# GpSimd's product with C in a selective scan: one instruction per unit of two steps instead of one per step

## The chip, the cores and the metric

The kernel runs on one core of one Trainium2 chip. The metric is device time in microseconds from start to end of one launch. The core has four computing engines with queues of their own: TensorE (PE), VectorE (DVE), ScalarE (ACT) and GpSimd (POOL). SyncE (SP) issues most transfers. An engine works its queue strictly in order; between engines only semaphores order the work.

## The reference, cut to what matters

Two layers run one after the other on a tensor of 32 x 96 x 56 x 56, all in f32. The first is a 7x7 depthwise convolution with a layer norm and an MLP. The second cuts the image into windows of 8 x 8 pixels and runs a two-dimensional selective scan in each, in four directions:

```
def step(h, inp):
    u_l, d_l, B_l, C_l = inp
    dA = jnp.exp(d_l[..., None] * A)
    h = h * dA + (d_l * u_l)[..., None] * B_l[:, :, None, :]
    y = jnp.einsum('bkdn,bkn->bkd', h, C_l)
    return (h, y)
```

Here d is 192 channels, n is 16 states per channel, k is 4 directions, and l runs over the 64 pixels of a window. delta (d_l) is softplus of a small product of the input. The change touches the product of h with C_l; its sum over n is another instruction.

## The kernel before, in words

**Tiles and turns.** layer0 comes first. layer1 then works on 196 tiles of 8 windows (512 pixels, `TOK`). Each engine has a function `body(b)`, which is one turn of 48 steps (`STEPS1`); turn b scans tile b, prepares parts of tile b+1, and finishes tile b-1. A turn has two phases (f = 0, 1: by rows and by columns) of 24 steps (`SPP`). Two successive steps, the even one and the odd one (s = 0, 1), are a unit; `unit(p)` gives a step's phase, its block J of 32 channels, its direction pair h, its slot and s. A unit's state, 128 x 2048 values, lies in one of six slots of the tile `state`.

**One step p, engine by engine.** ACT writes the decays exp(d A) into the slot four steps ahead (`decays`, L1256, two instructions a step). PE writes the step's inputs, 32 small matmuls, into one of two PSUM tiles dbu (`inputs`, L1032). It waits there for the scan of two steps before. DVE runs the recurrence in place over the 1024 columns of the step (`scan`, L1477). POOL multiplies these by C in place (`times_c`, L942); it waits for the step's scan and counts the product on `hc_done`. PE sums the states of a whole unit over n into the bank yb (`sum_states`, L1051), five steps after the unit's odd step (`LAG`); ACT copies the bank out. The sum counts on `ysum_done`, for which the decays of the unit six later wait.

**The chain of a step size.** Six times a turn (`CHAINS`, at steps 5, 12, 19, 33, 40 and 47) a block of 64 channels gets its delta. PE multiplies (`steps_of`, L1120) into the one bank pp that all side work shares; ACT takes absolute value, relu and exponential of it (`softplus`, L1325, L1326, L1328), then two logarithms (L1333, L1334). PE sums those three steps later (`exponent`, L1126) and ACT takes an exponential (`small_part`, L1339). Five steps after the chain's start, POOL adds (`step_size`, L949, counts `dl_done`), multiplies by u (`times_u`, L962 or L964, counts `hd_done`) and writes resets (L973, counts `reset_done`). The result goes through DRAM into dl, from which the decays are taken. PE transposes the product with u eight steps after the chain's start (`inputs_turned`, L1133) and ACT copies it (L1347) into du_t, which `inputs` reads. The softplus of a chain waits for `dl_done` of the chain before it. POOL also has one product a turn at step 35 (`gate`, L978).

**Where these sit in POOL's queue.** In step p, `times_c` comes first, then the chain's three instructions if p is 4, 10, 17, 24, 38 or 45, then at p = 35 the gate.

**Side work on pp.** The matmuls on pp go in a fixed order (`PP`). Each waits until the one before it has been read (`free_bank`), so L1100, the second depthwise convolution of the next tile (in steps 21 and 24, read by ACT in L1280, L1281, L1284), waits for L1347 of the transposition before it, and L1126 of step 22 waits for L1284.

**C and its loads.** SP brings C spread over partitions into cc, 2 h x 2 s x 1024 columns, a unit's 2048 columns of one h in one contiguous row (`c_rows`). It may overwrite a half h when `hc_done` shows that the last unit of that h in the phase is through (`LAST_STEP` = 18 for h = 0, 22 for h = 1). The first products of a phase on each h wait for the load (`cc_in`).

Of the kernel before, what the change touches and what calls it, by code (L numbers as in the profile page):

```python
# [7 lines left out]
ALU = mybir.AluOpType  # L8
# [33 lines left out]
WPS = TW // 2  # L42
# [5 lines left out]
LAST_STEP = [18, 22]  # L48
UPP = len(PHASE_J)
SPP = 2 * UPP  # L50
UNITS = 2 * UPP
STEPS1 = 2 * SPP
# [502 lines left out]
def layer1(nc, ln_g, ln_b, in_w, conv_w, conv_b, xproj_w, dt_w, dt_b, A_logs, Ds, on_g, on_b, out_w, alpha,  # L555
           act_d, base_d, cd, out, NT):
    ctx = ExitStack()
    with ctx:
        def sb(name, shape, dt=F32):
            return ctx.enter_context(nc.sbuf_tensor(name, shape, dt))  # L560
# [4 lines left out]
        def sem(name):  # L565
            return ctx.enter_context(nc.semaphore(name))
# [55 lines left out]
        cc = sb("cc", [128, 2, 2, STEP])  # L622

        state = sb("state", [128, NSLOT, TW, MG * WPX])
# [28 lines left out]
        cc_in = [sem(f"cc_in{h}") for h in range(2)]  # L653
# [10 lines left out]
        CCS = NG * 16  # L664
        STORES = TW * 16

        def later(t):
            return not (isinstance(t, int) and t == 0)
# [33 lines left out]
        def unit(p):  # L702

            f, of_phase = p // SPP, p % SPP // 2
            return f, PHASE_J[of_phase], PHASE_H[of_phase], p // 2 % NSLOT, p % 2
# [30 lines left out]
        with nc.Block() as block:  # L736

            @block.sync
            def _(sp):
# [10 lines left out]
                with nc.allow_non_contiguous_dma(reason="small weights, once"):  # L750
# [7 lines left out]
                    for part, (rows, first) in enumerate(PARTS):  # L758
                        its = slice(first, first + rows)
# [81 lines left out]
                def c_rows(T, f, h):  # L841

                    phase = T * 2 + f
                    if h == 0:
                        sp.wait_ge(cd_in[f], T * CDS + CDS)
                    if later(phase):
                        sp.wait_ge(hc_done, phase * SPP + (LAST_STEP[h] + 2 - SPP))
                    for g in range(NG):
                        src = cd[f, h].rearrange("s w g m t -> g (s w) (m t)")[g]
                        sp.dma_start(cc[JC * g:JC * g + JC, h, :, :].rearrange("p s (w x) -> p (s w) x", w=WPS),  # L850
                                     src.unsqueeze(0).broadcast_to([JC, TW, MG * WPX])).then_inc(cc_in[h], 16)

                def body(b):
                    if has(b):
                        c_rows(b, 0, 1)
# [7 lines left out]
                    if has(b):  # L863
                        both_halves(b, 1, 1)
                        c_rows(b, 1, 0)
                        c_rows(b, 1, 1)
                        both_halves(b, 1, 2)
# [29 lines left out]
            def _(pool):  # L897
# [37 lines left out]

                def times_c(b, p):
                    f, _, h, slot, s = unit(p)
                    pool.wait_ge(scan_done, b * STEPS1 + p + 1)
                    if p % SPP in (0, 4):
                        pool.wait_ge(cc_in[h], (b * 2 + f + 1) * CCS)  # L940
                    its = state[:, slot, WPS * s:WPS * s + WPS, :].rearrange("p w x -> p (w x)")
                    nc.gpsimd.tensor_tensor(its, its, cc[:, h, s, :], ALU.mult).then_inc(hc_done, 1)  # L942

                def step_size(T, f, j):

# [34 lines left out]
                def body(b):  # L980
                    for p in range(STEPS1):
                        if has(b):
                            times_c(b, p)
                        for T, f, j in chains_at(b, p, L_U):
                            step_size(T, f, j)
                            times_u(T, f, j)
                            reset(T, f, j)
                        if p == S_GATED and has(b - 1):
                            gate(b - 1)
# [10 lines left out]
            def _(pe):  # L1000
# [41 lines left out]
                def sum_states(T, p):  # L1042

                    f, J, h, slot, _ = unit(p)
                    bank = yb[J % 2]
                    pe.wait_ge(hc_done, T * STEPS1 + p + 1)
                    if h == 0 and (later(T) or 6 * f + J > 1):
                        pe.wait_ge(ye_done, T * (2 * NJC) + 6 * f + J - 1)
                    for m in range(MG):
                        src = state[:, slot, :, m * WPX:m * WPX + WPX].rearrange("p (q k) t -> p k q t", k=2)  # L1050
                        last = nc.tensor.matmul(bank[JC * m:JC * m + JC, :].rearrange("p (k q t) -> p k q t", k=2, t=WPX),  # L1051
                                                mask[:], src[:, ::-1, ::-1, ::-1] if h else src, start=h == 0, stop=h == 1)
                    if f == 0 and h == 0:
                        for m in range(MG):
                            its = slice(128 * m, 128 * m + 128)
                            last = nc.tensor.matmul(bank[JC * m:JC * m + JC, its],
                                                    skip_l[:, J // 2, JC * (J % 2):JC * (J % 2) + JC],
                                                    u[0:JB, J // 2, its], start=False, stop=False)
                    last.then_inc(ysum_done, 1)
# [145 lines left out]
                def body(b):  # L1205
                    for p in range(STEPS1):
                        T, q = (b, p + 1) if p < STEPS1 - 1 else (b + 1, 0)
                        done = b if p >= LAG else b - 1
                        if has(T):
                            inputs(T, q, 0)  # L1210
                        if has(done) and (p - LAG) % 2:
                            sum_states(done, (p - LAG) % STEPS1)
                        if has(T) and NE > 1:
                            first_halves_written(T, q)
                            inputs(T, q, 1)
                        front(b, p)
# [348 lines left out]
```

## Time and profile before

| | us |
|---|---|
| median of 3 runs | 31036.96 (31032.65 to 31046.93) |
| span of the profiled execution | 31035.4 |

No separate time of the profiled execution is on record; its span, from the first to the last instruction, lies within the three runs. Times in the views are microseconds from the start of that span. Busy is the share of the span in which an engine ran something; a line of a timeline merges neighbouring instructions of one line of code (x2, x6), with the idle time ahead of them in brackets and the engine and line whose end closed it. PE's share of 92% counts modelled ends of pipelined matmuls. Layer0 fills roughly the first 3.4 ms, in which POOL is idle nearly throughout.

### The profile page before, as it was taken

The page shows a single profiled execution, that of the slowest core. Times are in us where ns is not written, and L with a number is a line of the kernel's source. Part 1 is how long each engine was busy: PE and PEld are TensorE (multiplying, and loading weights), DVE is VectorE, ACT ScalarE, POOL GpSimd, SP SyncE. Part 2 cuts the span into 40 slices and gives each one's busy share as a digit, 9 for nine tenths or more (in the row PEclk, how much of TensorE's full clock was granted, in tenths as well). Part 3 has the DMA queues.
Part 4 walks back from the last instruction along what each step waited for, and adds up shares of the span by engine and source line. Part 5 has one row for each costly group of instructions (what it writes and reads, how often), then busy time and mean ns, then how long its engine had stood idle before and what let it go on. Part 6 is the DMA issues. An engine that isn't in the chain of part 4 may idle for free.

```text
span 31035.4 us, 986155 instructions
## 1 busy us (share of the span) xinstructions
PE 28615.5 (92%) x399070; PEld 10807.2 (35%) x399070; DVE 27602.9 (89%) x18447; ACT 24152.4 (78%) x37826; POOL 25853.7 (83%) x13288
## 2 busy tenths in 40 slices
PE   8999799999999999999999999999999999999998
PEld 2333233333333333333333333333333333333333
DVE  7888799999999999999999999999999999999998
ACT  4555688888888888888888888888888888888887
POOL 0000599999999999999999999999999999999999
PEclk9999999999999999999999999999999999999999
DMA  3333344444444444444444444444444444444444
GB/s 82 88 84 82 79 103 99 102 98 102 99 101 100 100 100 100 101 100 102 99 102 100 101 99 101 99 103 98 103 98 102 100 102 99 102 98 102 98 102 90
DMA packets 3821867, 3043.32 MB, mean 98 GB/s; under 512 B 2184848, under 2 KB 2987792, under 8 KB 3796944
## 3 DMA queue, kind: packets, MB, share of 16 engines
q1 hardware_dynamic: 3809888, 2910.77, 44.4%
q8 instruction: 3312, 54.26, 0.8%
q0 software_dynamic: 8560, 77.41, 0.7%
q14 instruction: 107, 0.88, 0.0%
HBM read 2325.71 MB, written 449.58 MB: 89 GB/s over the span
## 4 chain that ended last, share of the span: by engine, by line
PE 28%; POOL 20%; issue 18%; ACT 13%; DVE 8%; DMA 1%; POOLq 0%; SPq 0%; ACTq 0%; DVEq 0%
POOL state L942 17%; PE dbu L1032 9%; PE pp L1126 7%; DVE state L1477 5%; ACT state L1256 5%; PE yb L1051 4%; DVE dg L1467 2%; PE pp L1100 2%; POOL dd L949 2%; PE pp L1089 1%; PE pp L1120 1%; ACT sp_w L1333 1%; POOL dd L962 1%; ACT sp_v L1334 1%; PE b_t L1068 1%
## 5 line engine op out<-in xcount | busy, mean ns | idle before, releaser
L942 POOL TENSOR_TENSOR state<-state,cc 128x1024 f32<-128x1024 f32 x9408 | 22044.2, 2375 | 1411.5 <-DVE state L1477 1381.9
L1477 DVE TENSOR_TENSOR_SCAN state<-state,dbu 128x1024 f32<-128x1024 f32 x9408 | 21000.9, 2269 | 2295.8 <-PE dbu L1032 2292.6
L1256 ACT ACTIVATE state<-dl,a_neg 128x512 f32<-128x512 f32 x18816 | 12250.6, 711 | 21.2 <-DMA dl<-dlx 1.4
L1032 PE MATMUL dbu<-dg,du_t 64*32 64x256 f32 x301056 | 10198.2, 383 | 968.5 <-DVE state L1477 895.6
L1032 PEld LDWEIGHTS dbu<-dg,du_t 64*32 64x32 f32 x301056 | 5100.0, 106 | 7276.9 <-issue 6198.1
L1051 PE MATMUL yb<-state,mask 128*32 128x512 f32 x37632 | 5078.5, 612 | 2.2 <-POOL state L942 2.2
L1467 DVE TENSOR_TENSOR dg<-b_t,mask_q 128x1024 f32<-128x1024 f32 x3136 | 3757.7, 1198 | 41.4 <-PE b_t L1068 41.4
L229 POOL DMA_DIRECT2D act_d<-acted x32 | 16.3, 509 | 3218.2 <-DVE mixed L489 2909.2
L1126 PE MATMUL pp<-sp_a,minus 128*128 128x512 f32 x2352 | 1321.4, 644 | 587.4 <-ACT ye L1284 252.1
L1339 ACT ACTIVATE sp_y<-pp 128x512 f32<-128x512 f32 x1176 | 704.2, 599 | 1440.4 <-PE pp L1126 1417.1
L437 DVE SCALAR_TENSOR_TENSOR acc<-image,cw_v,acc 96x432 f32<-96x432 f32 (+2 forms) x2912 | 1687.6, 647 | 0.0
L262 PE MATMUL conv_p<-shifted,cw 128*32 128x424 f32 (+3 forms) x12096 | 1646.1, 542 | 0.4 <-DVE b1g L406 0.4
L949 POOL TENSOR_TENSOR dd<-sp_r,sp_y 128x512 f32<-128x512 f32 x1176 | 1507.9, 1282 | 111.3 <-ACT sp_y L1339 111.3
L1051 PEld LDWEIGHTS yb<-state,mask 128*32 128x32 f32 x37632 | 743.7, 108 | 1962.1 <-issue 1783.5
L1120 PE MATMUL pp<-xd,dt_l 128*128 128x512 f32 x2352 | 1324.4, 645 | 102.9 <-ACT xd L1308 81.5
L1126 PE MATMUL pp<-sp_w,minus 128*128 128x512 f32 x2352 | 1202.8, 593 | 0.0
L1126 PE MATMUL pp<-sp_v,minus 128*128 128x512 f32 x2352 | 1202.5, 593 | 0.0
L1347 ACT ACTIVATE du_t<-pp 128x512 f32<-128x512 f32 x1176 | 683.7, 581 | 541.2 <-PE pp L1133 540.6
L1325 ACT ACTIVATE sp_a<-pp 128x512 f32<-128x512 f32 x1176 | 698.9, 594 | 516.2 <-POOL dd L949 271.3
L1100 PE MATMUL pp<-xs,cw 96*32 96x448 f32 (+1 forms) x7056 | 1009.1, 563 | 12.7 <-DMA xs<-ye 9.1
L1308 ACT ACTIVATE xd<-pp,one_row 64x512 f32<-64x512 f32 x784 | 535.6, 683 | 608.4 <-PE pp L1109 603.4
L964 POOL TENSOR_TENSOR dd<-dd,u 128x512 f32<-128x512 f32 x588 | 902.7, 1535 | 92.7 <-POOL dd L949 62.1
(174 smaller groups left out, 26584.2 us busy)
## 6 DMA issues: line engine op xcount, KB each, us to landing
dl<-dlx SPq DMA_DIRECT2D x4704, 256.0 KB, 4.7
cc<-cd SPq DMA_DIRECT2D x3136, 256.0 KB, 6.2
dlx<-dd SPq DMA_DIRECT2D x1176, 256.0 KB, 2.0
shifted<-in_x SPq DMA_DIRECT2D x384, 392.0 KB, 12.5
xs<-ye SPq DMA_DIRECT2D x1176, 112.0 KB, 2.8
xs<-ye SPq DMA_DIRECT2D x588, 128.0 KB, 2.6
image<-in_x SPq DMA_DIRECT2D x32, 1176.0 KB, 24.5
act_d<-acted POOLq DMA_DIRECT2D x32, 1176.0 KB, 9.1
```

The source lines that it names most:

```text
L262: last = nc.tensor.matmul(dst[:, :, lo:hi], cw[:, cb * PCOLS + w, :], src.rearrange("p (i j) -> p i j", j=W)[:, :, lo + e:hi + e], start=t ...
L437: nc.vector.scalar_tensor_tensor(dst, src, weight, dst, ALU.mult, ALU.add).then_inc(tap_done, 1)
L942: nc.gpsimd.tensor_tensor(its, its, cc[:, h, s, :], ALU.mult).then_inc(hc_done, 1)
L949: nc.gpsimd.tensor_tensor(dd[:, 0, :], sp_r[:], sp_y[:], ALU.add).then_inc(dl_done, 1)
L1032: last = nc.tensor.matmul(dst[:, :, TQ * e:TQ * e + TQ], du_t[its, j, col:col + JC], dg[its, h, 2 * k + s, MG * TQ * g:MG * TQ * g + MG * ...
L1051: last = nc.tensor.matmul(bank[JC * m:JC * m + JC, :].rearrange("p (k q t) -> p k q t", k=2, t=WPX), mask[:], src[:, ::-1, ::-1, ::-1] if ...
L1100: last = nc.tensor.matmul(windows(pp[32 * q:32 * q + 32, :])[:, :, :, a:c], cw[:, 3 * cb + d, :], windows(xs[:, 2 * (cb % 3) + cb // 3, :] ...
L1120: nc.tensor.matmul(pp[:], dt_l[:, f, j, :], xd[:, f, :], start=True, stop=True).then_inc(pp_ready, 1)
L1126: last = nc.tensor.matmul(pp[:], minus[:, i, :], part[:], start=i == 0, stop=i == 2)
L1256: nc.scalar.activation(state[:, slot, :, m * WPX:m * WPX + WPX].rearrange("p (q k) t -> p q k t", k=2), by_place(dl[:, J // 2, 2 * h + J % ...
L1467: nc.vector.tensor_tensor(dg[:, h, blk, :].rearrange("p (n t) -> p n t", t=TQ), b_t[:, col:col + NS].unsqueeze(2).broadcast_to([128, NS, TQ]),
L1477: nc.vector.tensor_tensor_scan(its, its, dbu[p % 2][:], 0.0, ALU.mult, ALU.add).then_inc(scan_done, 1)
```

## The change

`times_c` does nothing on an even step. On an odd step it waits for the scan of that step (so for both), and multiplies the unit's 2048 columns by the 2048 columns of C in one instruction. `hc_done` counts units instead of steps; the two places that wait for it (`c_rows` on SP, `sum_states` on PE) count units too, and wait for the same data as before. The waits for `cc_in` move from steps 0 and 4 of a phase to steps 1 and 5.

```diff
@@ c_rows
                     if later(phase):
-                        sp.wait_ge(hc_done, phase * SPP + (LAST_STEP[h] + 2 - SPP))
+                        sp.wait_ge(hc_done, phase * UPP + (LAST_STEP[h] // 2 + 1 - UPP))
@@ times_c
                     f, _, h, slot, s = unit(p)
+                    if s == 0:
+                        return
+                    if p % SPP in (1, 5):
+                        pool.wait_ge(cc_in[h], (b * 2 + f + 1) * CCS)
                     pool.wait_ge(scan_done, b * STEPS1 + p + 1)
-                    if p % SPP in (0, 4):
-                        pool.wait_ge(cc_in[h], (b * 2 + f + 1) * CCS)
-                    its = state[:, slot, WPS * s:WPS * s + WPS, :].rearrange("p w x -> p (w x)")
-                    nc.gpsimd.tensor_tensor(its, its, cc[:, h, s, :], ALU.mult).then_inc(hc_done, 1)
+                    its = state[:, slot, :, :].rearrange("p w x -> p (w x)")
+                    nc.gpsimd.tensor_tensor(its, its, cc[:, h, :, :].rearrange("p s x -> p (s x)"),
+                                            ALU.mult).then_inc(hc_done, 1)
@@ sum_states
-                    pe.wait_ge(hc_done, T * STEPS1 + p + 1)
+                    pe.wait_ge(hc_done, T * UNITS + p // 2 + 1)
```

## Rows read from the trace of the kernel before

**Rows 1.** The page: busy us (share of span) and instructions of each engine.

```profile
PE 28615.5 (92%) x399070; PEld 10807.2 (35%) x399070; DVE 27602.9 (89%) x18447; ACT 24152.4 (78%) x37826; POOL 25853.7 (83%) x13288
```

**Rows 2.** The page: shares of the chain that ended last, by line.

```profile
POOL state L942 17%; PE dbu L1032 9%; PE pp L1126 7%; DVE state L1477 5%; ACT state L1256 5%; PE yb L1051 4%; DVE dg L1467 2%; PE pp L1100 2%; POOL dd L949 2%; PE pp L1089 1%; PE pp L1120 1%; ACT sp_w L1333 1%; POOL dd L962 1%; ACT sp_v L1334 1%; PE b_t L1068 1%
```

**Rows 3.** POOL's groups: shapes, xcount | busy us, mean ns | idle before, releasers.

```profile
L942 POOL TENSOR_TENSOR state<-state,cc 128x1024 f32<-128x1024 f32 x9408 | 22044.2, 2375 | 1411.5 <-DVE state L1477 1381.9 <-DMA cc<-cd 23.4
L949 POOL TENSOR_TENSOR dd<-sp_r,sp_y 128x512 f32<-128x512 f32 x1176 | 1507.9, 1282 | 111.3 <-ACT sp_y L1339 111.3
...
L973 POOL TENSOR_TENSOR dd<-resets 128x8 f32<-128x8 f32 x1176 | 245.1, 208 | 176.0 <-POOL dd L962 89.5 <-POOL dd L964 63.9 <-ACT state L1256 6.5
```

**Rows 4.** Line L978, once a turn: duration min/median/max ns, first and last start.

```profile
L978 POOL TENSOR_TENSOR yf<-yf,z x196: 2340/2365/2394, 3700.0 to 31021.8; 128x1024 f32<-128x1024 f32 x196
```

**Rows 5.** Waits over the span: waiter, releaser, us in total, times, longest.

```profile
ACT sp_a L1325 <- POOL dd L949: 271.3, 198, 3.2
```

**Rows 6.** Timeline of POOL in one turn, steps 3 to 17: start, duration.

```profile
11895.22 4.70 POOL L942 TENSOR_TENSOR state<-state,cc 128x1024 f32<-128x1024 f32 x2 [0.94 <-DVE state L1477]
11899.88 1.27 POOL L949 TENSOR_TENSOR dd<-sp_r,sp_y 128x512 f32<-128x512 f32 x1
...
11902.92 14.01 POOL L942 TENSOR_TENSOR state<-state,cc 128x1024 f32<-128x1024 f32 x6
11916.89 1.29 POOL L949 TENSOR_TENSOR dd<-sp_r,sp_y 128x512 f32<-128x512 f32 x1
...
11920.18 16.36 POOL L942 TENSOR_TENSOR state<-state,cc 128x1024 f32<-128x1024 f32 x7
11936.49 1.28 POOL L949 TENSOR_TENSOR dd<-sp_r,sp_y 128x512 f32<-128x512 f32 x1
11937.93 1.56 POOL L964 TENSOR_TENSOR dd<-dd,u 128x512 f32<-128x512 f32 x1 [0.16 <-PE pp L1120]
```

**Rows 7.** Timeline of DVE, same turn: scans 3 and 4, scan 17, scan 24.

```profile
11892.86 4.46 DVE L1477 TENSOR_TENSOR_SCAN state<-state,dbu 128x1024 f32<-128x1024 f32 x2
...
11929.08 2.29 DVE L1477 TENSOR_TENSOR_SCAN state<-state,dbu 128x1024 f32<-128x1024 f32 x1 [1.45 <-PE dbu L1032]
...
11952.95 2.29 DVE L1477 TENSOR_TENSOR_SCAN state<-state,dbu 128x1024 f32<-128x1024 f32 x1 [1.65 <-PE dbu L1032]
```

**Rows 8.** Timeline of ACT, same turn: softplus of steps 5 and 19, then L1347.

```profile
11901.25 0.60 ACT L1325 ACTIVATE sp_a<-pp 128x512 f32<-128x512 f32 x1 [1.31 <-POOL dd L949]
...
11937.92 0.60 ACT L1325 ACTIVATE sp_a<-pp 128x512 f32<-128x512 f32 x1 [0.26 <-PE pp L1120]
...
11941.28 0.58 ACT L1347 ACTIVATE du_t<-pp 128x512 f32<-128x512 f32 x1
```

**Rows 9.** Timeline of PE, same turn, steps 16 to 23.

```profile
11928.73 1.07 PE L1051 MATMUL yb<-state,mask 128*32 128x512 f32 x8
...
11940.25 0.66 PE L1133 MATMUL pp<-ident,dd 128*128 128x128 f32 x4
11941.53 1.10 PE L1032 MATMUL dbu<-dg,du_t 64*32 64x256 f32 x32 [0.63 <-DVE state L1477]
11942.56 2.57 PE L1100 MATMUL pp<-xs,cw 96*32 96x512 f32 x24
...
11948.80 1.12 PE L1126 MATMUL pp<-sp_a,minus 128*128 128x512 f32 x2 [1.29 <-ACT ye L1284]
```

**Rows 10.** Timeline of ACT in the rest of the same turn, step 32.

```profile
11980.67 1.38 ACT L1308 ACTIVATE xd<-pp,one_row 64x512 f32<-64x512 f32 x2 [1.25 <-PE pp L1109]
```

**Rows 11.** Timeline of PE in the rest of the same turn, step 43.

```profile
12008.37 1.12 PE L1126 MATMUL pp<-sp_a,minus 128*128 128x512 f32 x2 [0.71 <-ACT zi L1315]
```

**Rows 12.** Timeline of DVE, scan of the same turn's last step.

```profile
12019.19 2.29 DVE L1477 TENSOR_TENSOR_SCAN state<-state,dbu 128x1024 f32<-128x1024 f32 x1 [0.26 <-PE dbu L1032]
```

**Rows 13.** Timeline of DVE, scan of step 3 in a longer turn.

```profile
12596.14 2.28 DVE L1477 TENSOR_TENSOR_SCAN state<-state,dbu 128x1024 f32<-128x1024 f32 x1
```

**Rows 14.** Timeline of ACT, softplus of step 19 in that longer turn.

```profile
12642.38 0.60 ACT L1325 ACTIVATE sp_a<-pp 128x512 f32<-128x512 f32 x1 [0.26 <-PE pp L1120]
```

## The prediction

> **What bounds the kernel now.** I read the page's busy line first. PE is at 92%, DVE 89%, POOL 83%, ACT 78% [rows 1]; no engine is full, so the time is set by hand-overs inside a turn, not by one sum of busy time. The span holds 196 turns; the gate runs once in each, from 3700.0 to 31021.8 us [rows 4], so a turn takes 27,321.8 / 195 = 140.1 us. Whatever the change does, it does about 196 times, and 1 us a turn is 196 us.
>
> Then the chain's lines. POOL's product has the largest share, 17% [rows 2]. This must not be read as 17% to be won or lost. Over the whole span DVE is what POOL waits for, 1381.9 us [rows 3]; an engine that is often early is not the one that sets the pace. What counts are the points where another engine waits for POOL. The list of waits has one of any size: ACT's softplus for the `step_size`, 271.3 us in 198 waits, about one a turn [rows 5]. The timelines of one turn show which: the softplus of step 5 starts at 11901.25, after 1.31 us of idle that POOL ends [rows 8], as POOL's L949 ended at 11899.88 + 1.27 = 11901.15 [rows 6]. POOL's other wait in that place is for scan 3: it stands idle for 0.94 us, until scan 3 has ended at 11892.86 + 2.27 = 11895.13 [rows 6, 7]. So scan 3, two products, step size, softplus is a piece of the turn's pace.
>
> The second place is the softplus of step 19. It starts at 11937.92, put down to PE [rows 8], but POOL's L949 ended only at 11936.49 + 1.28 = 11937.77 [rows 6]: POOL is 0.15 us from being the bound. From 11895.22 to there POOL has no idle but the 0.16 us steps inside a chain's three instructions. Its work between scan 3 and step 17 is a solid block, and how long the new block is decides the result.
>
> **What one merged product costs.** The trace has no POOL product of 2048 columns. It has 128x512 at 1.282 us, 128x1024 at 2.375 and 128x8 at 0.208 [rows 3]. From 512 to 1024 columns is 1.093 us; twice that for 1024 more gives 2.375 + 2.186 = 4.561. The line from 8 to 1024 columns, 2.133 ns a column, gives 2.375 + 1024 x 2.133 ns = 4.559. I take 4.56. The bounds: from above twice today's, 4.75; from below, the slope of the two large shapes with no fixed part at all, 2048 x 2.135 ns = 4.37. Products in a row start closer than their duration: seven take 16.36 us [rows 6], so (16.36 - 2.375) / 6 = 2.33 each, 0.04 less than one lasts. A merged one then occupies 4.52 where a pair took 4.66, 0.14 less.
>
> The Trainium skill has a measured figure for just this shape: GPSIMD Engine Reference, section 3.1 (Elementwise, side-by-side cycle accounting), gives 4497 ns for a tensor_tensor of 2048 f32, an add. No row here shows it. By it the sum below would end at no loss a turn.
>
> **The change part by part.** POOL loses 4704 of 9408 products [rows 3], busy time 4704 x (2 x 2.375 - 4.56) = 890 us. None of it counts in itself, as POOL waits for DVE anyhow. What counts is when the consumers get their data.
>
> Step 4 (the known wait). Before, products 3 and 4 ran before the step size. Now step 4 has no product, and the unit of 2 and 3 starts after scan 3, at the same 11895.22, and lasts one merged product. L949 starts at 11895.22 + 4.52 = 11899.74 in place of 11899.88: 0.14 us earlier.
>
> Step 17 (the near miss). Here the chain sits in an odd step, right behind a merged product. Block before, from product 3: L949 at 11899.88, products again at 11902.92, L949 at 11916.89, products at 11920.18, L949 at 11936.49 [rows 6]. The chain's three instructions hold POOL 3.04 and 3.29 us. After: 11899.74 + 3.04 = 11902.78; three units (5, 7, 9), 13.56, to 11916.34; + 3.29 = 11919.63; four units (11 to 17), 18.08, to 11937.71. That is 1.22 us later than 11936.49. In words: the block holds eight whole units where it held fifteen products, so half a unit (2.33) comes in, the half that had been done while DVE scanned step 3, and eight savings of 0.14 go out. The scans don't hold this block: scan 17 ends at 11929.08 + 2.29 = 11931.37 [rows 7], the product of its unit starts at 11933.2.
>
> What follows it. L949 ends at 11938.99; with the 0.10 us that ACT took at step 5 the softplus starts at 11939.09, 1.17 after 11937.92. ACT is without a gap until L1347, so that ends at 11941.28 + 0.58 + 1.17 = 11943.03. `times_u` ends at 11937.93 + 1.56 + 1.22 = 11940.71, and PE's transposition, at 11940.25 before [rows 9], comes at about 11940.8 and is done before 11941.53, when PE starts the inputs it had waited 0.63 us for a scan to begin [rows 9]. So that wait swallows PE's part. ACT's part isn't swallowed whole: the convolution L1100 must not overwrite pp before L1347 has read it; it began at 11942.56 [rows 9], 0.70 after L1347's end, and would now begin at about 11943.10. Net: 1.22 - 0.05 - 0.70, plus 0.07 for the hand-over, = 0.54 us.
>
> Does this reach the end of the turn? L1100 releases ACT's four reads, L1284 releases L1126 after 1.29 us of idle on PE [rows 9], then come the inputs for scan 24, for which DVE idles 1.65 us [rows 7]. All of that moves by 0.54. Further on the hand-overs stay tight: ACT idle 1.25 for L1109, PE idle 0.71 for ACT's L1315, DVE idle 0.26 for PE ahead of scan 46 [rows 10 to 12]. I find no slack that gives it back, and scan 3 of the next turn starts the same block anew.
>
> Longer turns. PE's loop is written out eight turns at a time, and about one turn in eight (24) is longer. In one of them scan 3 ends at 12598.42 and the softplus of step 19 starts 43.96 later, at 12642.38 [rows 13, 14], in place of 42.79. The new L949 ends 43.86 after scan 3, so it costs nothing there. The sum: 172 turns x 0.54 = 93 us more, 24 x 0.14 = 3 us less: +90 us on 31,035.4, which is 31,125. The profiled span lies 1.6 us under the median of the runs, so no correction.
>
> **The edits at no cost.** The steps 10, 24, 38: their chains come at the same time or earlier, since they sit in even steps; step 45 is odd, and by the same sum its step size comes at most half a unit, 2.33 us, later. The 198 waits of softplus for L949 are one a turn and the one of step 5 is among them [rows 5, 8], so I take the softplus of step 47 to have room for it; if it had none, 1 us a turn more. `sum_states` takes the unit of 10 and 11 at 11928.73 [rows 9]; its product ends at 11919.63 + 4.56 = 11924.19, 4.5 us ahead. If that cover went, each of 24 sums a turn would stop PE. The `cc` reload waits for the same unit, which is done 1 us later and has its load needed one scan later; SP's queue behind it (the next chain's store) then waits no longer either. The decays hang on the sums and don't move.
>
> **The rivals.**
> 1. Not slower: the merged product is shorter than 4.49. Every 0.01 us counts eight times in the block, so the 0.54 is gone when a unit lasts 0.0675 less, 4.49; the place is L1347's 0.70 us ahead of L1100. Below it the gain is what step 4 wins, 2 x 2.33 less the unit's spacing: at 4.37, 0.33 us a turn, 65 us, 30,970. Against: three shapes of this trace on one line at 4.56. At 4.49 itself the time is 31,035 to 31,000. 18%, of which 8% for more than 62 us. (The Trainium skill's figure of GPSIMD Engine Reference, section 3.1, lies on this point.)
> 2. The instruction saves nothing (4.75). The block grows by 8 x 0.19 = 1.5 more: 2.05 us x 172 = 350 us: 31,390. For it only that a fixed part may be charged per 1024 columns. 8%.
> 3. The delay is real but given back behind L1100, by a slack I don't see: 31,035. Against it stand the tight hand-overs [rows 10 to 12]. 17%.
> 4. A consumer of whole units becomes late after all (`sum_states`, or cc through SP's queue), once or twice a turn by about a us: + 200 to 400 us. Against it the 4.5 us. 7%.
> Forecast: 50%.
>
> **How the numbers follow.** A difference under 0.2%, 62 us, can't be told from none here. The forecast holds +90 with a spread of about 60 (0.04 us on the product is 55 us), so a third of it falls below 62. Slower: 0.36 + 0.08 + 0.07 + a little of the rest, 0.54; faster 0.09; same 0.37. The range leaves out the far part of rivals 2 and 4 and the lowest of rival 1: 30,995 to 31,280.
>
> **What would show it.** L942 has 4704 instructions of 128x2048 near 4.56 us. The wait of the softplus L1325 for L949 rises from one a turn to about two, and the new one is at step 19, near 1.2 us. In a usual turn L949 of step 17 ends 43.9 us after scan 3, and L1100 starts 0.07 us after L1347's end. PE's sums still don't wait for L942. Wrong would be: L1100 with slack left, a product off 4.56, or DVE idle ahead of scan 24 unchanged while the time moves.

## The result and the profile after

| | before | after |
|---|---|---|
| median of 6 runs, us | 31033.90 (31028.22 to 31046.93) | 31132.83 (31117.82 to 31145.84) |
| span of the profiled execution | 31035.4 | 31116.2 |

The changed kernel takes 1.0029 times as long, 95% interval 1.0020 to 1.0039. The forecast was 31,125. First the page of the changed kernel: busy time by engine, the lines of the chain that ended last, and the group of POOL's product. POOL's product is now L944; line numbers past `times_c` have moved by three (L952 is `step_size`, L1480 the scan).

```profile
PE 28631.3 (92%) x399070; PEld 10810.1 (35%) x399070; DVE 27607.9 (89%) x18447; ACT 24139.7 (78%) x37826; POOL 25167.9 (81%) x8584
...
PE dbu L1035 9%; POOL state L944 8%; PE pp L1129 8%; ACT state L1259 7%; DVE state L1480 7%; PE yb L1054 4%; DVE dg L1470 3%; PE pp L1103 2%; PE pp L1123 2%; POOL dd L952 1%; PE pp L1111 1%; PE pp L1112 1%; ACT xd L1311 1%; ACT du_t L1350 1%; ACT sp_w L1336 1%
...
L944 POOL TENSOR_TENSOR state<-state,cc 128x2048 f32<-128x2048 f32 x4704 | 21347.2, 4559 | 2182.7 <-DVE state L1480 2172.2
```

POOL has 686 us less to do than in [rows 1] and waits 790 us longer for DVE than in [rows 3]; its share of the chain fell from 17% [rows 2] to 8%. By each of these three numbers the change looks like a gain, and the kernel is slower. The list of waits (waiter, releaser, us in total, times, longest) has the one that grew:

```profile
ACT sp_a L1328 <- POOL dd L952: 414.6, 319, 2.9
```

Against [rows 5] that is 121 more waits and 143 us more. Sorted by step, two things hide in this number: the softplus of step 19 waited for POOL once in the whole span before and now does in 187 of 196 turns, and that of step 5 does in 131 turns instead of 196. The timelines of a usual turn show them. POOL, from the product of steps 2 and 3 to the step size of step 17 (start, duration, idle before in brackets):

```profile
12057.94 4.56 POOL L944 TENSOR_TENSOR state<-state,cc 128x2048 f32<-128x2048 f32 x1 [2.06 <-DVE state L1480]
12062.46 1.27 POOL L952 TENSOR_TENSOR dd<-sp_r,sp_y 128x512 f32<-128x512 f32 x1
...
12082.32 18.11 POOL L944 TENSOR_TENSOR state<-state,cc 128x2048 f32<-128x2048 f32 x4
12100.36 1.30 POOL L952 TENSOR_TENSOR dd<-sp_r,sp_y 128x512 f32<-128x512 f32 x1
```

DVE in the same turn, scans 3 and 4:

```profile
12055.58 4.46 DVE L1480 TENSOR_TENSOR_SCAN state<-state,dbu 128x1024 f32<-128x1024 f32 x2
```

Scan 3 ends at 12055.58 + 2.27 = 12057.85, and the step size of step 17 at 12101.66, which is 43.81 us later; before it was 11937.77 - 11895.13 = 42.64 [rows 6, 7]. Before the change POOL stood idle twice, 0.92 us ahead of product 2 and 0.94 ahead of product 3, and did product 2 while DVE scanned step 3:

```profile
11891.91 2.37 POOL L942 TENSOR_TENSOR state<-state,cc 128x1024 f32<-128x1024 f32 x1 [0.92 <-DVE state L1477]
```

Now it stands idle once, for 2.06 us, about the same in all, and product 2 is inside the merged one, behind scan 3: that is the half unit that came into the block. ACT and PE behind the block:

```profile
12101.75 0.60 ACT L1328 ACTIVATE sp_a<-pp 128x512 f32<-128x512 f32 x1 [1.52 <-POOL dd L952]
...
12105.11 0.58 ACT L1350 ACTIVATE du_t<-pp 128x512 f32<-128x512 f32 x1
```

```profile
12104.11 1.10 PE L1035 MATMUL dbu<-dg,du_t 64*32 64x256 f32 x32
12105.82 2.57 PE L1103 MATMUL pp<-xs,cw 96*32 96x512 f32 x24 [0.61 <-ACT du_t L1350]
```

The softplus of step 19, put down to PE before [rows 8], now idles 1.52 us for POOL. The convolution L1103 (L1100 before), which had no idle [rows 9], stands 0.61 us until L1350 has read pp. Over the usual turns (median) scan 24 starts 58.36 us after the end of scan 3, before 57.82, and from scan 24 to the next turn's scan 0 it is 70.01 and 70.02: in such a turn the 0.54 us arise between scans 3 and 24 and nothing behind gives them back. The median turn goes from 140.06 to 140.58 us.

### The profile page after: what moved, and what is told of

The parts are those of the page before. It is cut to its first block, busy times and chain, and to the rows that moved or that the text cites. A ratio compares the mean times of both kernels' runs of the same rounds, so it can differ in the third digit from the quotient of the medians.

```text
span 31116.2 us, 980775 instructions
## 1 busy us (share of the span) xinstructions
PE 28631.3 (92%) x399070; PEld 10810.1 (35%) x399070; DVE 27607.9 (89%) x18447; ACT 24139.7 (78%) x37826; POOL 25167.9 (81%) x8584
## 4 chain that ended last, share of the span: by engine, by line
PE 31%; ACT 19%; issue 17%; DVE 11%; POOL 11%; ACTq 0%; DVEq 0%; SPq 0%; POOLq 0%; DMA 0%
PE dbu L1035 9%; POOL state L944 8%; PE pp L1129 8%; ACT state L1259 7%; DVE state L1480 7%; PE yb L1054 4%; DVE dg L1470 3%; PE pp L1103 2%; PE pp L1123 2%; POOL dd L952 1%; PE pp L1111 1%; PE pp L1112 1%; ACT xd L1311 1%; ACT du_t L1350 1%; ACT sp_w L1336 1%
## 5 line engine op out<-in xcount | busy, mean ns | idle before, releaser
L944 POOL TENSOR_TENSOR state<-state,cc 128x2048 f32<-128x2048 f32 x4704 | 21347.2, 4559 | 2182.7 <-DVE state L1480 2172.2
L1480 DVE TENSOR_TENSOR_SCAN state<-state,dbu 128x1024 f32<-128x1024 f32 x9408 | 21004.8, 2269 | 2358.3 <-PE dbu L1035 2355.4
L952 POOL TENSOR_TENSOR dd<-sp_r,sp_y 128x512 f32<-128x512 f32 x1176 | 1503.7, 1279 | 110.9 <-ACT sp_y L1342 110.9
L1350 ACT ACTIVATE du_t<-pp 128x512 f32<-128x512 f32 x1176 | 682.0, 580 | 556.7 <-PE pp L1136 556.7
L1103 PE MATMUL pp<-xs,cw 96*32 96x448 f32 (+1 forms) x7056 | 1009.2, 563 | 103.7 <-ACT du_t L1350 90.9
L1136 PE MATMUL pp<-ident,dd 128*128 128x128 f32 x4704 | 772.6, 287 | 290.5 <-ACT sp_r L1329 169.3
```

Source lines behind the costliest of these rows:

```text
L944: nc.gpsimd.tensor_tensor(its, its, cc[:, h, :, :].rearrange("p s x -> p (s x)"), ALU.mult).then_inc(hc_done, 1)
L952: nc.gpsimd.tensor_tensor(dd[:, 0, :], sp_r[:], sp_y[:], ALU.add).then_inc(dl_done, 1)
L1103: last = nc.tensor.matmul(windows(pp[32 * q:32 * q + 32, :])[:, :, :, a:c], cw[:, 3 * cb + d, :], windows(xs[:, 2 * (cb % 3) + cb // 3, :] ...
L1480: nc.vector.tensor_tensor_scan(its, its, dbu[p % 2][:], 0.0, ALU.mult, ALU.add).then_inc(scan_done, 1)
```

## The experiments

Each kernel was timed in five rounds beside the kernel before; ratios are to that, with 95% intervals.

**Only the block merged** (`in_block`), and **only the rest merged** (`out_block`). The edit lets `times_c` choose; a merged unit counts two on `hc_done`, so all waits keep their numbers. Counting two has a small price of its own: with all units merged POOL's program has 4,696 more semaphore instructions than the changed kernel's, and the step size of step 17 ends 0.10 us later (43.91 us after scan 3 against 43.81).

```diff
+                    whole = 2 <= p < 18        # out_block: p >= 18
+                    if whole and s == 0:
+                        return
...
+                    if whole:
+                        its = state[:, slot, :, :].rearrange("p w x -> p (w x)")
+                        nc.gpsimd.tensor_tensor(its, its, cc[:, h, :, :].rearrange("p s x -> p (s x)"),
+                                                ALU.mult).then_inc(hc_done, 2)
```

> Only the units of steps 2 to 17 are one instruction; all other steps keep one product each, and hc_done counts steps, so PE's and SP's programs are those of before. Theory (the solid block of POOL between scan 3 and the step size of step 17 is half a unit longer): the whole loss is here, +70 to +115 us against before, ratio about 1.003; the step size of step 17 ends 43.8 us after scan 3. Rival A (PE's register instructions for the new count): no loss, within 20 us of before. Rival B (consumers of whole units outside the block, cc reloads or the odd chain of step 45): half of the loss or less.

> Only the units of steps 18 to 47 are one instruction; steps 0 to 17 keep one product each, counts as before. Theory: no loss, within 20 us of before, though POOL loses 15 of 24 pairs a turn and its busy time falls by some 550 us. Rival B (a consumer of whole units outside the block, or the chain of step 45): +50 to +115 us. Rival A: no loss either.

`in_block`: 31108.56 us, ratio 1.0025 (1.0015 to 1.0034); step size of step 17 at 43.91 us after scan 3. With 8 of 24 units merged the loss is 80 us, as with all of them and the same counting (82, `all_by_two` below). `out_block`: 31386.70 us, 1.0117 (1.0102 to 1.0132), 358 us more than before, which no theory expected. The group of single products shows a releaser that had 23.4 us before [rows 3]:

```profile
L950 POOL TENSOR_TENSOR state<-state,cc 128x1024 f32<-128x1024 f32 x3528 | 8257.0, 2370 | 595.6 <-DVE state L1485 396.5 <-DMA cc<-cd 196.7
```

So the reload of cc is late, for product 4 of a turn, and with it the step size of step 4 (7.24 us after scan 3 in the median turn, before 6.03). The wait for cc is 173 us longer, half of the 358; what makes the rest is seen in the next run.

**Where the late reload comes from.** `out_mid` merges steps 18 to 43 and leaves 44 to 47 single:

```diff
-                    whole = p >= 18
+                    whole = 18 <= p < 44
```

> As the kernel that merges only the units of steps 18 to 47 (which took 358 us more than before), but the last two units of the turn, steps 44 to 47, keep one product a step; merged are steps 18 to 43. Theory C (the 358 us are the reload of cc for h = 1: it goes out behind the transfers of step 45's chain, which a merged unit ahead of it makes 1.2 us later, and product 4 of the next turn, alone in its instruction, needs it at once): no loss, within 25 us of before. Rival D (merged units outside the block cost by themselves, each sum or reload a little): 13 of the 15 units are still merged, so +250 us or more.

31356.44 us, 1.0101 (1.0086 to 1.0117). Theory C in this form fell: the last units were not it. But the test had left the chain of step 45 late, since merged units still stood ahead of it. POOL's timeline in `out_mid`, around a scan 0 that starts at 12131.67:

```profile
12143.97 2.38 POOL L950 TENSOR_TENSOR state<-state,cc 128x1024 f32<-128x1024 f32 x1 [0.59 <-DVE state L1485]
12147.83 2.36 POOL L950 TENSOR_TENSOR state<-state,cc 128x1024 f32<-128x1024 f32 x1 [1.49 <-DMA cc<-cd]
...
12166.19 2.37 POOL L950 TENSOR_TENSOR state<-state,cc 128x1024 f32<-128x1024 f32 x1 [1.35 <-DVE state L1485]
```

The first wait makes the second. Product 4 is late, so the softplus of step 5 is, so PE's work on pp and its inputs are (DVE idles 6.28 us for them ahead of scan 10, in the turn of rows 6 it was 3.11), and POOL waits 1.35 us for a scan in the middle of the block, where it had no idle before [rows 6]. From scan 3 to the end of step 17's step size it is 44.27 us in the median turn, before 42.64.

SP's queue of the same turn: store of the chain and reload of cc.

```profile
12131.73 0.34 SPq L825 DMA_DIRECT2D dlx<-dd  x1
12137.67 1.79 SPq L850 DMA_DIRECT2D cc<-cd  x4
```

The same two before the change, in a turn whose scan 0 starts at 12022.96:

```profile
12021.63 0.34 SPq L825 DMA_DIRECT2D dlx<-dd  x1
12027.01 1.79 SPq L850 DMA_DIRECT2D cc<-cd  x4
```

The store leaves 1.4 us later in the turn, the reload 2 us later (6.0 us into the turn against 4.05; over the turns the medians are 5.69 and 4.00). `out_mid_45` takes only that away: the chain of step 45 stands ahead of product 45.

```diff
-                        if has(b):
+                        if has(b) and not (p == 45):
                             times_c(b, p)
                         for T, f, j in chains_at(b, p, L_U):
                             ...
+                        if has(b) and (p == 45):
+                            times_c(b, p)
```

> Still merged in steps 18 to 43 and single elsewhere (which took 324 us more than before), with one reordering: step 45's chain of three POOL instructions comes ahead of product 45. In that run merged units ahead of the chain had left its reset 1.4 us later than before, its store, its loads and, behind them in SP's queue, the reload of cc 2 us later, and product 4 waited for cc. Theory C' (so it is this chain, not the last unit): the reset comes 1 us earlier than before the change, the reload goes out by 5.5 us into the turn, the waits of POOL for cc go, time within 30 us of before. Rival D (merged units outside the block cost by themselves): +250 us or more.

31031.41 us, 0.9999 (0.9990 to 1.0008), and 13 of 24 units are merged. POOL's wait for cc is back to 15.9 us:

```profile
L950 POOL TENSOR_TENSOR state<-state,cc 128x1024 f32<-128x1024 f32 x4312 | 10094.2, 2376 | 231.6 <-DVE state L1487 214.9 <-DMA cc<-cd 15.9
```

The reload goes out 4.73 us into the median turn. So merged units outside the block cost nothing that these runs resolve (6 us less than before, inside the interval), and the late chain of step 45 does if the first use of cc stays at step 4. In the changed kernel the unit of 4 and 5 starts after the first step size and isn't held up: L944 above has no wait for cc. Nor has `all_by_two`, where the reload leaves as late as in `out_mid`, at 5.91 us.

**The order at step 17** (`chain17_first`: the edit of `out_mid_45`, with 17 for 45, in the changed kernel).

> The changed kernel with one reordering in POOL's queue: in step 17 the chain's three instructions come ahead of the unit's product instead of behind it. Theory: the step size of step 17 comes a unit (4.5 us) earlier, PE is again what the softplus of step 19 waits for, the loss of 0.54 us a turn goes and the 0.14 us of step 4 stays: 20 to 30 us under before, about 31,005. Rivals A and B: still +60 to +115 us against before.

31020.46 us, 0.9998 (0.9989 to 1.0007), and the step size of step 17 ends 39.30 us after scan 3. The loss is gone: 8 us under before, where 20 to 30 were expected, and the interval can't tell these apart. The median turn, 139.99, is 0.07 under that of before, where 0.14 was expected.

**PE's own instructions** (`all_by_two`). The changed `sum_states` makes PE compute a count of its own; the changed kernel runs 4,368 more register instructions there. Here `whole = True` and counts of two leave PE's program as it was.

> As the changed kernel, every unit one instruction, but each counts two on hc_done, so that PE and SP wait for the same numbers and run the same programs as before the change (the changed kernel has some 4,400 more register instructions on PE). Theory: the loss stays, +70 to +115 us, same as the changed kernel. Rival A: it goes, within 20 us of before; a part of it going would be PE's part.

31111.41 us, 1.0026 (1.0016 to 1.0036); median turn 140.66. The loss stays, so most of it isn't PE's. A part may be. PE's pauses ahead of the inputs that no releaser explains (issue) are 77.3 us in 52 waits in the changed kernel, 10.3 in 30 here:

```profile
PE dbu L1035 <- issue: 77.3, 52, 4.0
```

Most fall on step 5, where the softplus then waits for PE in place of POOL. By the medians this kernel is 21 us shorter than the changed one, inside the intervals, though its block is 0.10 us longer by the way it counts, which at 0.10 us a turn would be up to 20 us. So an estimate of PE's part is 20 to 40 us of the 99; no run shows it by itself.

**Half a unit out of the block** (`split_first`: `whole = p // 2 != 1`).

> Every unit one instruction except that of steps 2 and 3, which keeps one product a step. Theory (half a unit too much in POOL's block from scan 3 to step 17): product 2 is done while DVE scans step 3, the step size of step 4 comes about 2.1 us earlier than before the change and that of step 17 about 0.8 us earlier, the loss is gone and PE, not POOL, is waited for at step 5; the gain there ends where PE itself is busy, 0.7 us a turn: 100 to 160 us under before, about 30,900. Rival: if the loss comes from merged units anywhere else, it stays, +60 us or more.

30887.71 us, 0.9953 (0.9939 to 0.9966), as expected. One unit of 24 done in two steps turns a loss of 99 us (82 with the same counting) into a gain of 145: step 4's step size ends 4.09 us after scan 3 where it ended at 6.03 before the change, and step 17's at 42.07 where it was 42.64.

**A dose of POOL time**, one idle product of 128x512, inside the block and outside it:

```diff
                         for T, f, j in chains_at(b, p, L_U):
                             ...
+                        if p == 7 and has(b):      # dose_out: p == 29
+                            nc.gpsimd.tensor_tensor(idle[:], idle[:], idle[:], ALU.mult)
```

> The changed kernel with one idle POOL product of 128x512, about 1.24 us, added after product 7, inside the block from scan 3 to the step size of step 17; it writes a tile of its own. Theory: the block is the turn's pace, so the whole of it counts, 1.24 x 196 = 243 us on the changed kernel, at most 250 and at least 200: 31,320 to 31,375. Rival (the place was a coincidence): under 60 us.

> The same idle product after product 29, where POOL waits for DVE in every turn. Theory: nothing, within 25 us of the changed kernel, about 31,125. Rival (POOL's busy share counts anywhere, or DVE suffers beside it): +100 to +243 us.

`dose_in`: 31299.42 us, 1.0085 (1.0071 to 1.0098). `dose_out`: 31123.29 us, 1.0027 (1.0017 to 1.0038), the changed kernel's time. The same instruction costs 167 us over the changed kernel in the one place (176 over the other dose) and nothing in the other. The size was missed: 31,320 at least was expected, 200 us. The dose was taken from another product of that shape, at 1.282 us [rows 3], and it is shorter here:

```profile
L995 POOL TENSOR_TENSOR idle<-idle 128x512 f32<-128x512 f32 x196 | 205.1, 1046 | 0.0
```

It holds POOL for 1.00 us (the step size of step 17 ends 44.81 us after scan 3 in place of 43.81), and in the profiled executions the median turn is longer by 1.01: one for one. These two lie further apart than the medians, for `dose_in`'s was the slowest of its five and the changed kernel's the fastest of six: their spans differ by 200 us, and by the medians the dose is worth 0.85 to 0.90 us a turn.

**Chains ahead of the products**, at a lag of four steps, in the changed kernel (`early_whole`) and in the kernel before (`early_steps`):

```diff
-L_LOG, L_SUM, L_U = 1, 3, 5
+L_LOG, L_SUM, L_U = 1, 3, 4
...
-                        if has(b):
-                            times_c(b, p)
                         for T, f, j in chains_at(b, p, L_U):
                             ...
+                        if has(b):
+                            times_c(b, p)
```

> The changed kernel with each chain's three POOL instructions placed four steps after the chain's start in place of five, and ahead of that step's product. Theory: the step sizes of steps 4 and 17 leave POOL's block altogether; the softplus of steps 5 and 19 wait for PE only; 0.7 us a turn under before as PE is busy until then: 100 to 180 us under before, about 30,900. Rival (what was lost was not the place behind the products): no more than the reordered step 17 gave, within 30 us of before.

> The kernel before the change (one product a step) with the same earlier places for the chains' three POOL instructions. Theory: the gain is that of the places, not of the merged product: the same time as the changed kernel with early places within 30 us, about 30,900. Rival (the merged product is worth its 890 us of POOL busy time once it is not in the way): the merged one is faster by 50 us or more.

`early_steps`: 30883.02 us, 0.9951 (0.9937 to 0.9964), the fastest of all, 150 us under before. `early_whole`: 30973.49 us, 0.9981 (0.9972 to 0.9990). The places give the gain, and against the changed kernel the earlier places are worth 159 us; but with merged products it is 90 us less than with single ones, which neither theory had. In both the softplus waits for POOL once in the whole span. What differs is PE. In `early_whole` a group of inputs early in the turn is broken by such a pause (issue); in `early_steps` the same group runs through:

```profile
12022.44 0.64 PE L1037 MATMUL dbu<-dg,du_t 64*32 64x256 f32 x9 [0.46 <-DVE state L1482]
12023.49 1.06 PE L1037 MATMUL dbu<-dg,du_t 64*32 64x256 f32 x23 [0.41 <-issue]
```

```profile
11999.61 1.10 PE L1034 MATMUL dbu<-dg,du_t 64*32 64x256 f32 x32 [0.46 <-DVE state L1479]
```

Over the span such pauses are 68.8 us in 115 waits in `early_whole`, and 20.4 us in 19 in `early_steps` (lists of waits):

```profile
PE dbu L1037 <- issue: 68.8, 115, 3.7
```

```profile
PE dbu L1034 <- issue: 20.4, 19, 2.6
```

`early_by_two` is `early_whole` with counts of two, which gives PE the program of before (and POOL its 4,696 semaphore instructions more).

> The changed kernel with the chains' three instructions at the earlier places, but with counts of two on hc_done, so that PE's program is that of before the change. Theory E (early_whole, at 30,973, missed the 30,883 of the kernel with single products because PE's program carries some 4,400 more register instructions and shows more gaps inside its inputs early in the turn): within 25 us of 30,883. Rival F (the merged product itself costs something at another place): it stays at 30,950 to 30,990.

30887.22 us, 0.9952 (0.9939 to 0.9966). The loss against single products, 86 of the 90 us, went with the counting by units, not with the product. What the counting changes is PE's program and POOL's, and POOL's got longer, so PE's extra instructions are what is left. The pauses are 54 us less (14.5 in 17 waits here). Those of `early_whole` fall nearly all on steps 5 and 8, and on five of each eight successive turns (tiles 2 to 6 modulo 8). In tiles 4 and 5 it is 58.0 us there from scan 3 to scan 24, in `early_steps` 57.02. PE's loop is written out eight turns at a time, so the pauses go with the place in its program. What makes them the traces don't show.

## Why the prediction was right

- The merged product at 4.56 us: measured 4.559.
- POOL's busy time less by 890 us: the group lost 697, and no time hung on it. The 890 counted whole durations, while products in a row overlap by 0.04 us; with the 0.14 that the prediction itself used for the block it is 4704 x 0.14 = 659.
- Step 4's step size 0.14 earlier: it starts 4.52 us after the product, before 4.66. Worth less in time than said (`chain17_first`).
- The block 1.22 us longer, the step size 43.86 after scan 3: measured 43.81. That the place is the cause is shown by `in_block`, `split_first`, `chain17_first` and the two doses, from four sides: merged there alone, half a unit out, the chain moved ahead, time added inside and outside.
- The 0.70 us of slack ahead of L1100 are used up and 0.54 us of the delay are left over: L1103 starts 0.13 us after L1350's end (0.07 was said), and scan 24 is 0.54 later.
- No slack behind: in the trace `dose_in`'s 1.00 us came out as 1.01 a turn. In the mean over all turns 0.04 us a turn, 7 us in all, are won behind scan 24, in the last two of each eight turns; rival 3 is true to that small size.
- The longer turns: 0.14 us less each was forecast. The wait of step 19 is in these turns too. In the turns of the kind that the prediction read in rows 13 and 14, one of eight, scan 3 to scan 24 became 0.47 us shorter, from 58.95 to 58.48 in the mean, and scan 0 to scan 3 became 0.57 us longer, from 14.77 to 15.34. Together 0.10 more: near nothing, as said, but by two movements that the sum doesn't have.
- The size. The mean turn (turns 6 to 190) rose by 0.44 us, x 196 = 86, the profiled spans by 81, the medians of six runs by 99; the sum had said 90. Of these 86, some 80 arise between scans 3 and 24, some 14 between scans 0 and 3, and some 7 are won back behind scan 24. So the mechanism is the one forecast, and that its sum comes within 10 us of the measured time is in part luck: PE's part, the pause ahead of scan 3 and the gain in the longer turns are not in it and cancel in part.
- The chances: half of the weight with a third of it below 62 us is 0.33, not 0.36; the 0.54 for slower is then nearer 0.50.
- What it cost at nothing and shouldn't have: "the cc reload waits for the same unit, ... and has its load needed one scan later; SP's queue behind it then waits no longer either". In the change the reload does leave later (4.67 us into the median turn, before 4.00), because step 45's chain does (its reset 1.2 us later), and the later first use hides it, as `all_by_two` shows at 5.91 us. `out_block` and `out_mid` took that use back to step 4 and lost 358 and 324 us. The conclusion held, the reason was half of it.
- What it didn't count: PE's register instructions. In this change their part can't be told from the noise (20 to 40 us by the estimate above), and it is 86 us where POOL no longer holds the softplus (`early_whole` against `early_by_two`).

Of the rivals, a shorter product (4.49 was its condition) falls with 4.559, a product without saving likewise, and a give-back behind L1100 with the equal 70.01 and 70.02 us from scan 24 on. Late reloads fall because L944 has no wait for cc, and late sums because PE's weight loads for them wait less for POOL's product than before: 72.0 us in 162 waits, before 178.7 in 427.

## What to carry to other kernels

Merging two instructions saves a fixed part each time, but the merged one can't start before its second input, so the half that used to lie beside the producer moves behind it. Find the solid blocks of an engine's timeline (no idle but the chain's own), take from each the consumer at its end, and count: instructions inside times the saving, against the half that comes in at the front. If the balance is wrong, move the small urgent instruction ahead of the bulky ones before changing the bulk: that, with one step less of lag, was worth 150 us here, without any merging.

## What wasn't expected of the hardware

- A POOL product of a 128x512 tile with itself, written back onto it, takes 1.046 us, where `step_size`, which adds two different inputs of that shape into a third tile, takes 1.282 [rows 3]. The tile was all zeros; which of these differences counts wasn't tried.
- POOL's instructions with two different inputs keep one line through 512, 1024 and 2048 columns: 1.282 (the sum of `step_size`), 2.375 and 4.559 us (the products), 2.13 ns a column.
- The time from the store of step 45's chain (256 KB) to its loads isn't fixed and doesn't follow the store's place: in the median turn 2.9 us before the change, 2.6 in the changed kernel, where the store leaves 1.2 us later in the turn, 3.6 in `all_by_two` with the store at the changed kernel's place, and 3.7 in `out_mid_45`, where it leaves 1 us earlier than before. So a delay of 1.4 us on POOL became 2 us on the reload behind it in one turn shown above; the cause is open.
- Some 22 register instructions more a turn in PE's program went with 86 us more in one kernel, 0.4 us a turn, as pauses ahead of and inside runs of matmuls; in the changed kernel the same pauses (77.3 us) went with at most some 40 us, where POOL held the next softplus back anyway.
